# The order of VectorE's work in token attention, and the preparation of its first chunk

## The chip, the cores and the metric

One core of a Trainium2 chip runs the whole program. Its engines are TensorE (matrix products, with the weight load as a separate step), VectorE, ScalarE, GpSimd and SyncE; each runs its own list of instructions in order, and the lists are tied together by semaphores that count up. Transfers are started by SyncE, and those that scatter rows by GpSimd. The metric is the time of one execution on the device in microseconds (us).

## The reference, cut to what matters

The input is 16 images of 128 channels and 16x16 pixels. Three blocks follow one another:

```python
x = conv_block(x)                      # attention over the images, batch norm, relu, conv3x3 (Wc), + x
t = tokens(x)                          # 16 images x 256 pixels, 128 features
z = layer_norm(t)
sq, sk, rv = z @ wq_s * scale, z @ wk_s, z @ wv_r          # 8 search heads, 2 retrieval values, d = 16
search = softmax(sq @ sk.T)                                # per image and head: 256 x 256
retrieved = search @ rv                                    # two values per head
gate = softmax over the two of (rq . (retrieved @ wk_ret))
t = t + (sum over the two of gate * retrieved) @ w_out
z2 = layer_norm(t)
top2 of z2 @ Wg over 8 experts, softmax of the two         # routing
t = t + sum over the two of share * silu(z2 @ W1[e]) @ W2[e]
```

## The kernel before, in words

The 4096 tokens are cut into 8 chunks of 512 (two images each). Everything up to the relu comes first and is not touched. Then `token_attention` runs: for chunk g it convolves (`conv_taps`, nine taps, three products each since every operand is split into a high and a low part), adds the input (`add_conv`, VectorE), turns the sum to tokens (`head_turn`), normalises it (`norm_stats`, `normalise`), turns it back, and makes keys, queries and token products (`head_k`, `head_q`, `head_tokens`). Keys and queries go through memory (`qk_rows`, the "bounce") and come back laid out by head (`k_stack`, `q_stack`; six and three transfers for each of the two images), all issued by SyncE in `stack`.

The order of all engines is written out by hand in `body(g)`, one per chunk, with the same step names on every engine. A body has two halves, one for each image b of chunk g, of eight steps s (one head each). In a step TensorE makes `shifted_scores(g, b, s)` of this image and `scores` of the image that comes next; VectorE takes the maximum of each row of these scores (`row_max`, L1280). TensorE has two banks for `scores`, so scores s waits for row maximum s-2. After the eight steps VectorE splits the maxima in high and low (`split_max`, last instruction L1293), TensorE turns them (`turn_max`, L1605), VectorE and ScalarE place them as four extra rows of `q_stack` (`place_max`, L1298), and only then can the next half's shifted scores start. The exponent is ScalarE's; `retrieve` on TensorE multiplies by the values.

Between the row maxima, VectorE does the rest of its work in a fixed order. In the first half of body g (from chunk 2 on; chunk 1 has no routing yet):

- s = 1, 2, 3: `retrieve` parts 0, 1, 2 of chunk g-1 (the gate of the two values; part 2 writes `o_tok`, L1330 and L1334). TensorE needs `o_tok` at its step 4 for `tail_turn` (L1655), and through it the output projection.
- s = 2, 3, 4: `route` parts 0, 1, 2 of chunk g-2 (choice of two experts; L1359 to L1384), each behind the `retrieve` part of that step.
- s = 5: `add_attention` (L1341); s = 6: `norm_stats`; s = 7: `normalise_t2`.

In the second half: `row_max` of the next chunk's first image; behind the first one `add_conv(g + 2)` (L1242), which TensorE needs at its step 1 for `head_turn` (L1557); `retrieve` of chunk g at steps 1, 4, 5; statistics and normalisation at 3 and 4; at step 7 `place(g - 2)` (L1389 to L1408: six small instructions that turn the rank of each token among its expert's tokens into the row it is scattered to), then `split_max`. GpSimd waits for what `place` wrote (`rows_ready`) and scatters eight tiles of rows per chunk (L973). TensorE's `turn_max` at the end of this half writes the bank that `place` reads first, and waits for that (`spot_read`).

Body 6 has no convolution left, body 7 is written out apart (`last_body`). At the end the experts run, once all rows are scattered.

Ahead of body 0 stands the preparation of chunk 0: `stack(0, 0)` on SyncE, `scores(0, 0, s)` on TensorE with the same two banks, and `row_max(0, 0, s)`, with `add_conv(2)` behind the fourth. TensorE has the last tap of chunk 2's convolution behind its first scores. ScalarE's images 12 to 15 (`image_pair` 6 and 7) and VectorE's `low(12)` to `low(15)` stand ahead of the scores; the convolution of chunk 6 needs them four bodies later.

Of the kernel before, what the change touches and what calls it, by code (L numbers as in the profile page):

```python
# [22 lines left out]
PIX = HW * HW  # L23
# [683 lines left out]
def token_attention(nc, ctx, block, sb, sem, bank, pad_h, pad_l, resid, virt, ident, wc_h, wc_l, norm_a, norm_b, power, wq, wk,  # L707
# [170 lines left out]

    def chunk(tensor, g):
        return tensor[:, bass.ds(g * CH, CH)]  # L880

    @block.sync
    def _(sp):
        def stack(g, ring):
# [3 lines left out]
            def bounce(first, signal):  # L888

                sp.dma_start(qk_rows[bass.ds(g, 1), first:first + 2].rearrange("g n c t -> c (g n) t"),  # L890
                             f32(qk[:, first:first + 2, :])).then_inc(signal, 16)

            def fill_k(b):
                at = slice(b * PIX, (b + 1) * PIX)
                for slot, n in enumerate((0, 0, 1)):
                    src = qk_rows[bass.ds(g, 1), n, :, at].rearrange("g (p a r) t -> a r (g p) t", p=NP, a=2)
                    for a in range(2):
                        row = 32 * slot + D * a
                        sp.dma_start(f32(k_stack[row:row + D, ring, a:S:2, at]), src[a]).then_inc(stacked[b], 16)

            def fill_q(b):
                at = slice(b * PIX, (b + 1) * PIX)
                for slot, n in enumerate((2, 3, 2)):
                    src = qk_rows[bass.ds(g, 1), n, :, at].rearrange("g (p r) t -> r (g p) t", p=NP)
                    sp.dma_start(f32(q_stack[32 * slot:32 * slot + 32, ring, :, at]), src
                                 ).then_inc(stacked[b], 16)

            sp.wait_ge(k_ready, g + 1)
            bounce(0, k_bounced)
            sp.wait_ge(q_ready, g + 1)  # L910
            bounce(2, q_bounced)
            sp.wait_ge(k_bounced, 16 * (g + 1))
            fill_k(0)
            sp.wait_ge(q_bounced, 16 * (g + 1))
            fill_q(0)
            fill_k(1)
            fill_q(1)
# [4 lines left out]
        stack(0, 0)  # L922
# [75 lines left out]
    def _(act):  # L998
# [182 lines left out]

        keep_t(0)
# [4 lines left out]
        keep_tok(0, 0, 0)  # L1187
        keep_tok(0, 1, 0)
        image_pair(6)
        split_zt(1)  # L1190
# [23 lines left out]
    def _(dve):  # L1214
# [63 lines left out]
        def row_max(g, b, s):  # L1278
            dve.wait_ge(s_done, 2 * S * g + S * b + s + 1)
            nc.vector.tensor_reduce(s_max[:, :, s], ps_s[s % 2][:, :].rearrange("p (a j) -> p a j", a=2), AX.X,  # L1280
                                    ALU.max).then_inc(max_done, 1)
# [104 lines left out]
        def place(u, ring, src=ps_x):  # L1386
# [798 lines left out]
```

## Time and profile before

| what | value |
|---|---|
| time, median of 3 runs | 685.08 us (684.0 to 688.95) |
| the profiled execution | 685.38 us, span of the profile 683.6 us |
| mean granted TensorE clock | 0.927 of full speed |
| TensorE matmul busy | 566.0 us (83%) |
| VectorE busy | 475.9 us (70%) |
| ScalarE busy | 333.1 us (49%) |
| GpSimd busy | 262.6 us (38%) |
| first shifted scores of body 0 | 191.95 us |
| turns of `t_chunk` in bodies 1, 2, 3, 4 and 5 | 243.18, 280.30, 319.65, 357.59 and 395.47 us |
| first product of the experts | 500.40 us |

The profile is one execution. Its span is 1.78 us shorter than the time of that execution, which is 0.30 us above the median. Engines are named PE (TensorE), DVE (VectorE), ACT (ScalarE), POOL (GpSimd) and SPq (SyncE issuing transfers). In a timeline a row gives the start, the duration, engine, line, operation, what it writes and reads, and in brackets how long the engine was idle before it and what released it. DVE instructions overlap a little at their ends: a row maximum lasts 0.69 us, but the next instruction can start some 0.6 us after it. In a view by stretches each engine's busy time is followed by the number of its instructions.

### The profile page before, as it was taken

What the parts mean: (1) busy time and instruction counts of PE and PEld (TensorE: products, weight loads), DVE (VectorE), ACT (ScalarE), POOL (GpSimd) and SP (SyncE); (2) the same over time, 40 slices, a digit from 0 to 9 for tenths busy, and PEclk for the clock granted to TensorE, in tenths of its full rate; (3) what the DMA queues carried; (4) which work ended last, traced back from release to release, by engine and by line L of the source; (5) the groups of instructions that cost most, each with busy time, mean ns of one, the idle gap of its engine ahead of it and who ended that gap; (6) DMA issues with size and microseconds to landing.
All of it is one profiled execution on the core that took longest, in us unless ns stands there. A gap on an engine that the chain in (4) does not pass through costs nothing. (4 is left out here: it accounts for less than half of the span.)

```text
span 683.6 us, 10705 instructions
## 1 busy us (share of the span) xinstructions
PE 566.0 (83%) x3180; PEld 439.7 (64%) x3180; DVE 475.9 (70%) x1227; ACT 333.1 (49%) x718; POOL 262.6 (38%) x328
## 2 busy tenths in 40 slices
PE   5999999849788988979898887876169999999910
PEld 4888888636565767666666665654058888888810
DVE  6886774855557777777878778785537767767715
ACT  3322302233356465554636355544148888888800
POOL 3245443458000100141413314247603666666660
PEclk9999999959879999999999999998569999999965
DMA  7994145649531405041230505001278777776109
GB/s 262 365 347 145 57 170 185 203 164 372 153 116 39 155 1 155 1 151 36 96 92 31 157 3 184 9 25 48 76 251 293 234 243 230 246 235 221 51 6 363
DMA packets 55224, 105.46 MB, mean 154 GB/s; under 512 B 8744, under 2 KB 21689, under 8 KB 55040
## 3 DMA queue, kind: packets, MB, share of 16 engines
q1 hardware_dynamic: 50176, 96.24, 42.6%
q0 software_dynamic: 4992, 8.54, 3.6%
q8 instruction: 26, 0.43, 0.3%
q14 instruction: 30, 0.25, 0.1%
HBM read 58.15 MB, written 48.42 MB: 156 GB/s over the span
## 5 line engine op out<-in xcount | busy, mean ns | idle before, releaser
L1949 POOL DMA_INDIRECT y_slots<-virt,pad_l x92 | 95.7, 1041 | 72.5 <-DVE virt L2001 49.5
L1280 DVE TENSOR_REDUCE s_max<-bank 128x2 f32<-128x512 f32 x128 | 87.4, 689 | 40.3 <-PE bank L1596 39.8
L1059 ACT ACTIVATE s_expd<-bank 128x512 f32<-128x512 f32 x128 | 76.9, 602 | 53.5 <-PE bank L1617 52.3
L973 POOL DMA_INDIRECT x_slots<-rows,slot_of x64 | 63.1, 986 | 55.9 <-DVE rows L1408 38.3
L937 POOL TENSOR_TENSOR ln_rstd<-ln_var,power 128x4 f32<-128x4 f32 x17 | 17.4, 1026 | 173.4 <-DVE ln_var L1256 173.4
L1989 DVE TENSOR_TENSOR k_stack<-virt,k_stack 128x512 fp32r<-128x512 f32 x92 | 63.4, 689 | 24.9 <-ACT k_stack L1968 24.2
L1632 PE MATMUL bank<-s_expd,rvx 128*64 128x256 f32 x512 | 70.5, 397 | 1.5 <-ACT s_expd L1059 1.0
L61 PE MATMUL bank<-pad_h,u_h 128*128 128x512 f32 x144 | 59.9, 416 | 8.4 <-DVE pad_l L399 8.4
L1617 PE MATMUL bank<-q_stack,k_stack 100*128 100x256 f32 x256 | 61.8, 325 | 5.0 <-DVE q_stack L1298 5.0
L1968 ACT ACTIVATE k_stack<-virt 128x512 fp32r<-128x512 f32 x92 | 58.2, 633 | 10.1 <-PE bank L63 7.2
L1963 ACT ACTIVATE virt<-bank 128x512 f32<-128x512 f32 x92 | 55.0, 597 | 14.3 <-PE bank L63 13.9
L1596 PE MATMUL bank<-k_stack,q_stack 96*128 96x256 f32 x256 | 55.5, 303 | 3.9 <-DMA q_stack<-qk_rows 2.3
L63 PE MATMUL bank<-pad_h,u_l 128*128 128x512 f32 x144 | 58.0, 403 | 0.0
L62 PE MATMUL bank<-pad_l,u_h 128*128 128x512 f32 x144 | 57.9, 402 | 0.0
L1617 PEld LDWEIGHTS bank<-q_stack,k_stack 100*128 100x128 f32 x256 | 43.0, 199 | 18.0 <-DVE q_stack L1298 7.0
L1596 PEld LDWEIGHTS bank<-k_stack,q_stack 96*128 96x128 f32 x256 | 42.5, 204 | 6.2 <-DVE s_max L1280 2.8
L1632 PEld LDWEIGHTS bank<-s_expd,rvx 128*64 128x64 f32 x512 | 31.5, 138 | 22.6 <-ACT s_expd L1059 5.1
L1066 ACT ACTIVATE ret_f<-bank 128x256 f32<-128x256 f32 x64 | 24.4, 382 | 39.8 <-PE bank L1632 39.8
L61 PE MATMUL bank<-k_stack,pad_h 128*128 128x512 f32 x92 | 40.5, 440 | 0.0
L1984 DVE TENSOR_TENSOR k_stack<-bank,k_stack 128x512 fp32r<-128x512 f32 x23 | 15.9, 692 | 30.5 <-ACT k_stack L1958 30.5
L61 PEld LDWEIGHTS bank<-pad_h,u_h 128*128 128x128 f32 x144 | 27.8, 193 | 14.3 <-issue 8.3
L62 PE MATMUL bank<-k_stack,pad_h 128*128 128x512 f32 x92 | 36.7, 399 | 0.0
(260 smaller groups left out, 1321.8 us busy)
## 6 DMA issues: line engine op xcount, KB each, us to landing
x_slots<-blank SPq DMA_DIRECT2D x8, 2112.0 KB, 17.3
pad_h<-w_split SPq DMA_DIRECT2D x23, 512.0 KB, 4.4
q_stack<-w_split SPq DMA_DIRECT2D x23, 512.0 KB, 5.7
qk_rows<-qk SPq DMA_DIRECT2D x16, 512.0 KB, 3.0
k_stack<-qk_rows SPq DMA_DIRECT2D x96, 64.0 KB, 2.4
q_stack<-qk_rows SPq DMA_DIRECT2D x48, 128.0 KB, 2.6
pad_l<-x_slots SPq DMA_DIRECT2D x23, 264.0 KB, 5.2
e_raw<-in_w SPq DMA_DIRECT2D x16, 256.0 KB, 3.0
```

The lines of the kernel that those rows point to most:

```text
L61: pe.matmul(out, w_h, x_h, start=start, stop=False)
L62: pe.matmul(out, w_h, x_l, start=False, stop=False)
L63: return pe.matmul(out, w_l, x_h, start=False, stop=stop)
L973: pool.indirect_dma_start(out=x_slots[:, :], out_offset=bass.IndirectOffsetOnAxis(ap=slot_of[:, ring, k, j:j + 1], axis=0), in_=rows[:, ri ...
L1059: nc.scalar.activation(expd[:, s % 4].rearrange("p a i -> p (a i)"), ps_st[s % 2][:, :], ACT.Exp).then_inc(exp_done, 1)
L1280: nc.vector.tensor_reduce(s_max[:, :, s], ps_s[s % 2][:, :].rearrange("p (a j) -> p a j", a=2), AX.X, ALU.max).then_inc(max_done, 1)
L1596: last = pe.matmul(ps_s[s % 2][:, i * PIX:(i + 1) * PIX], q_stack[0:96, ring, s // 2, at + i * P:at + (i + 1) * P], k_stack[0:96, ring, s, ...
L1617: last = pe.matmul(ps_st[s % 2][:, i * PIX:(i + 1) * PIX], k_stack[0:100, ring, s, at + i * P:at + (i + 1) * P], q_stack[0:100, ring, s // ...
L1632: last = pe.matmul(ps_pv[p % 2][h * RF:(h + 1) * RF, 0:PIX], rvx[:, ring, 2 * b + a, :], expd[:, 2 * (p % 2) + h, a, :], start=(a == 0), s ...
L1949: pool.indirect_dma_start(out=y_slots[:, :], out_offset=bass.IndirectOffsetOnAxis(ap=ids, axis=0), in_=y_rows[:, t % 2, j, :], in_offset=N ...
L1968: nc.scalar.activation(hid_h[:, f], hid[:, f], ACT.Copy).then_inc(hid_high, 1)
L1989: nc.vector.tensor_tensor(hid_l[:, f], hid[:, f], f32(hid_h[:, f]), ALU.subtract).then_inc(hid_ready, 1)
```

## The change

Five things, all in `token_attention`:

1. First half of a body: `retrieve` part 2 of chunk g-1 moves from step 3 to step 2, directly behind part 1. The three parts of `route` move from steps 2, 3, 4 to steps 4, 5, 6.
2. Second half: `add_conv` moves ahead of the first `row_max`.
3. `place` is cut in two. `place_spots` (its first instruction, the one that reads the bank) stays at step 7; `place_rows` (the other five) goes behind `split_max` and `place_max`, to the end of the body.
4. Chunk 0: its scores use four banks instead of two (`ps_s + ps_st`); TensorE makes the last tap of chunk 2's convolution ahead of them, and VectorE `add_conv(2)` ahead of all its row maxima. `low(12)` to `low(15)` move into steps 2 to 5 of body 0.
5. Chunk 0's transfers: SyncE bounces and lays out the keys alone (both images, 1 + 12 transfers); ScalarE bounces the queries between its two `keep_tok` and lays them out behind `split_zt(1)` (1 + 6 transfers), ahead of `image_pair(6)`.

```diff
     @block.sync
+        def first_stack():
+            sp.wait_ge(k_ready, 1)
+            bounce(sp, 0, 0, k_bounced)
+            sp.wait_ge(k_bounced, 16)
+            fill_k(sp, 0, 0, 0)
+            fill_k(sp, 0, 0, 1)
...
-        stack(0, 0)
+        first_stack()
         stack(1, 1)
...
     @block.scalar
+        def bounce_first_q():
+            act.wait_ge(q_ready, 1)
+            bounce(act, 0, 2, q_bounced)
+        def stack_first_q():
+            act.wait_ge(q_bounced, 16)
+            act.wait_ge(stack_init, 2 * S + 1)
+            fill_q(act, 0, 0, 0)
+            fill_q(act, 0, 0, 1)
...
         keep_tok(0, 0, 0)
+        bounce_first_q()
         keep_tok(0, 1, 0)
+        split_zt(1)
+        stack_first_q()
         image_pair(6)
-        split_zt(1)
         image_pair(7)
...
     @block.vector
-        def place(u, ring, src=ps_x):
+        def place_spots(u, src=ps_x):
...
+        def place_rows(u, ring):
             at, n = tiles_of(u), count_of(u)
             dve.wait_ge(spot_read, 4 * u + 1)
...
+                if stage == FIRST and s in (2, 3, 4, 5):
+                    low(10 + s)
                 if stage != FIRST:
-                    if s in (1, 2, 3):
+                    if s in (1, 2):
                         retrieve(g - 1, 1, s - 1)
+                    if s == 2:
+                        retrieve(g - 1, 1, 2)
                     if s == 5:
                         add_attention(g - 1)
...
-                if g >= 2 and s in (2, 3, 4):
-                    route(g - 2, ring, s - 2)
+                if g >= 2 and s in (4, 5, 6):
+                    route(g - 2, ring, s - 4)
...
             for s in range(S):
+                if stage == MIDDLE and s == 0:
+                    add_conv(g + 2)
                 if stage != LAST:
                     row_max(g + 1, 0, s)
-                if stage == MIDDLE and s == 0:
-                    add_conv(g + 2)
...
                 if g >= 2 and s == 7:
-                    place(g - 2, ring)
+                    place_spots(g - 2)
...
                 place_max(g + 1, 0, 1 - ring)
+            if g >= 2:
+                place_rows(g - 2, ring)
...
-        low(12)
-        low(13)
         low_zt(1)
-        low(14)
-        low(15)
+        add_conv(2, ps_pv[0])
         for s in range(S):
-            row_max(0, 0, s)
-            if s == 3:
-                add_conv(2, ps_pv[0])
+            row_max(0, 0, s, first_banks)
...
     @block.tensor
-            need(pe, max_done, 2 * S * g + S * b + s - 1)
+            need(pe, max_done, 2 * S * g + S * b + s + 1 - len(banks))
...
-        conv_taps(2, range(4, 8), ps_pv[0])
+        conv_taps(2, range(4, 9), ps_pv[0])
         head_k(1)
         for s in range(S):
-            scores(0, 0, s, 0)
-            if s == 0:
-                conv_taps(2, range(8, 9), ps_pv[0])
+            scores(0, 0, s, 0, first_banks)
```

`last_body` and what follows it keep their order; there `place` is only written as its two parts one behind the other.

## Rows read from the trace of the kernel before

**Rows 1.** Stretch, length, busy PE, PEld, DVE, ACT, POOL, PEclk, DMA: bodies 2, 4.
```profile
280.30:319.65 39.35, 35.03 (x227) 26.33 (x227) 29.97 (x99) 19.80 (x51) 10.87 (x13) 0.96 0.27 82
357.59:395.47 37.88, 33.54 (x226) 24.95 (x227) 29.79 (x99) 19.69 (x51) 10.88 (x13) 1.00 0.28 85
```

**Rows 2.** Timeline of TensorE: its waits for VectorE in bodies 1, 2 and 6.
```profile
228.30 0.63 PE L1655 MATMUL bank<-ident,o_tok 128*128 128x128 f32 x4 [0.72 <-DVE o_tok L1334]
...
265.42 0.63 PE L1655 MATMUL bank<-ident,o_tok 128*128 128x128 f32 x4 [1.82 <-DVE o_tok L1334]
...
276.52 0.38 PE L1605 MATMUL bank<-ident,m_split 128*128 128x128 f32 x2
...
280.30 0.65 PE L1557 MATMUL bank<-ident,t_chunk 128*128 128x128 f32 x4 [0.69 <-DVE t_chunk L1242]
...
292.91 0.41 PE L1605 MATMUL bank<-ident,m_split 128*128 128x128 f32 x2 [1.61 <-DVE m_split L1293]
...
440.57 0.41 PE L1605 MATMUL bank<-ident,m_split 128*128 128x128 f32 x2 [0.75 <-DVE m_split L1293]
```

**Rows 3.** Chain that ended last: the first scatter of the last body.
```profile
461.10 1.04 POOL x_slots L973
```

**Rows 4.** Timeline of VectorE in the first half of body 2.
```profile
262.62 0.18 DVE L1369 TENSOR_REDUCE best<-logits 128x4 f32<-128x32 f32 x1
...
263.73 0.69 DVE L1280 TENSOR_REDUCE s_max<-bank 128x2 f32<-128x512 f32 x1
264.34 0.41 DVE L1330 TENSOR_TENSOR prod<-prod,ret 128x256 f32<-128x256 f32 x1
...
265.19 0.18 DVE L1372 SCALAR_TENSOR_TENSOR other<-hot,logits 128x32 f32<-128x32 f32 x1
...
268.20 0.69 DVE L1280 TENSOR_REDUCE s_max<-bank 128x2 f32<-128x512 f32 x1 [0.37 <-PE bank L1596]
269.25 0.69 DVE L1341 TENSOR_TENSOR resid<-bank,resid 128x512 f32<-128x512 f32 x1 [0.35 <-PE bank L1661]
270.50 0.69 DVE L1280 TENSOR_REDUCE s_max<-bank 128x2 f32<-128x512 f32 x1 [0.57 <-PE bank L1596]
...
272.97 0.69 DVE L1280 TENSOR_REDUCE s_max<-bank 128x2 f32<-128x512 f32 x1 [0.38 <-PE bank L1596]
...
275.57 0.21 DVE L1293 TENSOR_TENSOR m_split<-s_neg,m_split 128x16 fp32r<-128x16 f32 x1
```

**Rows 5.** Busy time by stretch: the first half of body 6, without convolution.
```profile
412.00:425.00 13.00, 10.66 (x80) 7.57 (x78) 12.18 (x45) 7.20 (x21) 5.48 (x7) 1.00 0.70 215
```

**Rows 6.** Timeline of VectorE in the second half of body 2.
```profile
283.55 0.69 DVE L1280 TENSOR_REDUCE s_max<-bank 128x2 f32<-128x512 f32 x1 [1.00 <-PE bank L1596]
...
291.28 0.18 DVE L1389 TENSOR_TENSOR spot<-bank,first_row 128x32 f32<-128x32 f32 x1
...
292.18 0.17 DVE L1289 TENSOR_SCALAR s_neg<-s_max 128x16 f32<-128x16 f32 x1
```

**Rows 7.** Timeline: VectorE's first row maximum of body 6; GpSimd behind a scatter.
```profile
410.28 0.69 DVE L1280 TENSOR_REDUCE s_max<-bank 128x2 f32<-128x512 f32 x1 [0.83 <-PE bank L1596]
...
455.26 1.04 POOL L937 TENSOR_TENSOR ln_rstd<-ln_var,power 128x4 f32<-128x4 f32 x1 [4.46 <-DVE ln_var L1256]
```

**Rows 8.** Timeline of all engines in the preparation of chunk 0.
```profile
176.68 0.63 ACT L1030 ACTIVATE zt_h<-zt 128x512 fp32r<-128x512 f32 x1
...
177.62 1.37 SPq L905 DMA_DIRECT2D q_stack<-qk_rows  x3
...
181.41 0.60 PE L1596 MATMUL bank<-k_stack,q_stack 96*128 96x256 f32 x2 [2.34 <-DMA q_stack<-qk_rows]
...
189.45 0.17 DVE L1289 TENSOR_SCALAR s_neg<-s_max 128x16 f32<-128x16 f32 x1
...
190.82 0.37 ACT L1053 ACTIVATE q_stack<-bank 4x256 fp32r<-4x256 f32 x1 [11.91 <-PE bank L1605]
```

**Rows 9.** Busy time by stretch: the start of the second half of body 6.
```profile
428.00:430.00 2.00, 2.00 (x12) 1.77 (x10) 1.58 (x5) 1.38 (x4) 0.87 (x3) 0.50 0.00 0
```

More of the change, by code:

```diff
@@ L877, in max_bank, with bounce, fill_k @@
         return ps_x if stage in (FIRST, MIDDLE) else ps_conv
+    first_banks = ps_s + ps_st
     def chunk(tensor, g):
         return tensor[:, bass.ds(g * CH, CH)]
+    def bounce(queue, g, first, signal):
+        queue.dma_start(qk_rows[bass.ds(g, 1), first:first + 2].rearrange("g n c t -> c (g n) t"),
+                        f32(qk[:, first:first + 2, :])).then_inc(signal, 16)
+    def fill_k(queue, g, ring, b):
+        at = slice(b * PIX, (b + 1) * PIX)
+        for slot, n in enumerate((0, 0, 1)):
+            src = qk_rows[bass.ds(g, 1), n, :, at].rearrange("g (p a r) t -> a r (g p) t", p=NP, a=2)
+            for a in range(2):
+                row = 32 * slot + D * a
+                queue.dma_start(f32(k_stack[row:row + D, ring, a:S:2, at]), src[a]).then_inc(stacked[b], 16)
@@ L882, in _, with fill_q @@
+    def fill_q(queue, g, ring, b):
+        at = slice(b * PIX, (b + 1) * PIX)
+        for slot, n in enumerate((2, 3, 2)):
+            src = qk_rows[bass.ds(g, 1), n, :, at].rearrange("g (p r) t -> r (g p) t", p=NP)
+            queue.dma_start(f32(q_stack[32 * slot:32 * slot + 32, ring, :, at]), src
+                            ).then_inc(stacked[b], 16)
     @block.sync
     def _(sp):
-        def stack(g, ring):
[L888 to L906, printed above, removed]
@@ L908, in stack @@
+        def first_stack():
[4 more added lines that the diff above has]
+            fill_k(sp, 0, 0, 1)
+        def stack(g, ring):
             sp.wait_ge(k_ready, g + 1)
-            bounce(0, k_bounced)
+            bounce(sp, g, 0, k_bounced)
             sp.wait_ge(q_ready, g + 1)
-            bounce(2, q_bounced)
+            bounce(sp, g, 2, q_bounced)
             sp.wait_ge(k_bounced, 16 * (g + 1))
-            fill_k(0)
+            fill_k(sp, g, ring, 0)
@@ L1474, in last_body @@
             normalise_t2(g - 1, 0)
-            place(g - 2, ring)
+            place_spots(g - 2)
+            place_rows(g - 2, ring)
             for part in range(3):
@@ L1479, in last_body @@
                 route(g - 1, 0, part)
-            place(g - 1, 0)
+            place_spots(g - 1)
+            place_rows(g - 1, 0)
             add_attention(IMAGE_A)
@@ L1518, in _ @@
         route(IMAGE_A, 1, 2)
-        place(IMAGE_A, 1, ps_s[0])
+        place_spots(IMAGE_A, ps_s[0])
+        place_rows(IMAGE_A, 1)
         for part in range(3):
             route(IMAGE_B, 1, part)
-        place(IMAGE_B, 1, ps_s[1])
+        place_spots(IMAGE_B, ps_s[1])
+        place_rows(IMAGE_B, 1)
         dve.wait_ge(list_sums, 1)
@@ L1587, in head_tokens, with scores @@
                 last.then_inc(tok_done, 1)
-        def scores(g, b, s, ring):
+        def scores(g, b, s, ring, banks=ps_s):
             if s == 0:
                 pe.wait_ge(stacked[b], STACK * (g + 1))
-            need(pe, max_done, 2 * S * g + S * b + s - 1)
+            need(pe, max_done, 2 * S * g + S * b + s + 1 - len(banks))
             at = b * PIX
             for i in range(2):
-                last = pe.matmul(ps_s[s % 2][:, i * PIX:(i + 1) * PIX],
+                last = pe.matmul(banks[s % len(banks)][:, i * PIX:(i + 1) * PIX],
                                  q_stack[0:96, ring, s // 2, at + i * P:at + (i + 1) * P],
```

11 lines of the change are left out of this document (6 added, 5 removed).

## The prediction

> **What bounds the kernel now.** I read the views from the outside in. First the busy time of a whole body, from one turn of `t_chunk` to the next [rows 1]: body 4 lasts 37.88 us, in which TensorE works for 33.54 and VectorE for 29.79. The reader is to see that TensorE sets the pace and that at most its idle time, 4.34 us, can be won in a body. Body 2 is longer by 1.47 us at a mean clock of 0.96; that is a matter of the clock, below.
>
> Second, TensorE's waits in the timeline [rows 2]. In body 2 there are three, each for VectorE: 1.82 us for `o_tok`, 0.69 for `t_chunk`, 1.61 for the split maxima that end the body. Together 4.12, nearly the whole idle time. The same three stand, to 0.03 us, in bodies 2, 3, 4 and 5; body 1, which has no routing yet, waits 0.72 for `o_tok`, and body 6 waits 0.75 for the maxima that end it. Between 265.42 and 280.30 TensorE waits for nothing: it reaches the turn of the maxima at 276.52 without a wait.
>
> Third, the chain that ended last: attention ends with the scatters of GpSimd, and the chain enters them at 461.10 [rows 3], when VectorE in `last_body` has placed chunk 5. Behind it lie 8 + 8 + 4 + 4 scatters and the experts, none of which the change touches. So whatever VectorE and TensorE save before `last_body` goes to the end one to one.
>
> **Retrieval ahead of routing.** In body 2 `retrieve` part 2 starts at 264.34, behind routing's part 0 and a row maximum that begin at 262.62 [rows 4]. With both out of the way `o_tok` comes 1.72 us earlier, and TensorE, which waits 1.82, starts its turn at about 263.70.
>
> Not all of it is kept, because what stood ahead now stands behind, nearer to the end of the half. From 262.62 on VectorE has part 2 (264.34 to 265.19, 0.85), two row maxima that are ready (263.73 to 264.34, 0.61 each) and routing's part 0 (262.62 to 263.73, 1.11): it is through at 265.80. The next row maximum hangs on TensorE and comes 1.72 earlier than now, at 266.48; `add_attention` likewise at 267.53. After that routing's parts 1 and 2 fill what was waiting. So of the four waits 0.37, 0.35, 0.57 and 0.38 [rows 4], 1.67 in all, some 0.94 stays (the first two, the first of them longer: 0.59 + 0.35), and 0.73 goes. The split ends at 275.78 now, 0.73 earlier is 275.05, and 0.15 for the signal (o_tok's own delay) puts `turn_max` at 275.2, where TensorE alone would be there at 276.52 - 1.72 = 274.80. The half gets 1.32 shorter by this count; since neighbouring DVE instructions overlap by some 0.09 at each wait that goes, I take 1.4. Bounds: 1.72 if VectorE is never late, 0 if it becomes the bound, as body 6 shows it: there VectorE works 12.18 of 13.00 us [rows 5], and its order of work changes nothing, so I count no gain in body 6. Four bodies (2 to 5) give 5.6. In body 1 only a row maximum (0.61) leaves the front of part 2, against a wait of 0.72: 0.6. Sum 6.2.
>
> **Convolution's sum first.** It waits only for the convolution's last tap, which ends before TensorE begins the half; VectorE is then idle until the first scores arrive. The row maximum behind it is some 0.2 us late, but the scores that wait for it come two steps later. TensorE's 0.69 goes in bodies 1 to 5. That it lasts to the end of the half is seen at the fourth row maximum, where VectorE waits 1.00 for TensorE [rows 6]; from there on VectorE runs through to the split, so the chain simply starts earlier. 5 x 0.69 = 3.45.
>
> **Ranks in two parts.** From 291.28 to 292.18 `place` holds up the split by 0.90 [rows 6]. The spots stay (about 0.15 of it); 0.75 leaves, and TensorE's wait behind it is 1.61 (bodies 2 to 5) or 0.75 (body 6), so all of it counts: 5 x 0.75 = 3.75. The five moved instructions then stand ahead of the next body's first row maximum. What hides them is VectorE's wait there, 0.83 [rows 7]; without it each body would lose 0.75. The scatters start about 1.5 us later in a body. Behind them GpSimd waits 4.46 us for the next statistics [rows 7], and in the other bodies longer: hidden too.
>
> **Chunk 0.** Now the first scores start at 181.41 and the split at 189.45 [rows 8], 8.04 us, in which a convolution tap and `add_conv` stand between eight row maxima on two banks. With four banks and both of them ahead, VectorE has eight maxima in a row: 0.60 for the first product + 7 x 0.61 + 0.73 = 5.60, a gain of 2.4. The tap and the sum are hidden by the wait for the transfers (2.34 us of TensorE). The start depends on the third query transfer. SyncE issues three in 1.37 us from 177.62, so the third starts at 178.53 and TensorE 2.88 later. ScalarE comes to its three when `zt_h` is written, at 177.31 now; the bounce ahead delays it by an issue (0.46), image pair 6, now behind it, gives time back: it lies between 176.7 and 177.8, and I take 177.1. Third transfer 178.0, scores 180.9, 0.5 earlier. No row here has a transfer issued by ScalarE. Sum 2.9; bounds 4 (nothing but VectorE's eight maxima, at once) and 1.55 (the rival below). ScalarE's images 12 to 15 come some 5 us later (six issues of 0.46 and the wait for the bounce); what hides that is its 11.91 us of idle time ahead of `place_max` at 190.82 [rows 8]. The four `low` go into VectorE's waits for TensorE in body 0, of the kind and size of rows 4; not hidden they would cost 4 x 0.4 (an estimate from the 0.69 of a full-width row, for half the width).
>
> By the Trainium skill (Perfetto Trace Analysis, DMA Instruction — HWDGE) the block that generates descriptors is shared by the issuing engines and locked for one instruction at a time. By it the gain of this part would be the 1.55 of the rival below; no run here shows it yet.
>
> **The clock.** Body 2 has a mean granted clock of 0.96, body 4 with the same waits and the same work 1.00, and body 2 takes 1.47 longer [rows 1]: TensorE fell to the lower level, 1.2 GHz, for a while. The same is seen in body 6, behind the waits of its middle: 0.50 for 2 us [rows 9]. With half of the 1.61 of body 2 gone I count half of the 1.47: 0.7.
>
> **Sum.** 6.2 + 3.45 + 3.75 + 2.9 + 0.7 = 17.0. The profiled execution took 685.38 (span 683.6 and 1.78 around it), so 668.4; it lies 0.3 above the median, within the spread of the runs shown.
>
> **The rivals.** (a) VectorE becomes the bound of the first half, as in body 6: each `o_tok` wait turns into a wait for the split, and the 6.2 is lost: 674.6. For it speaks that VectorE's slack falls to under 1 us; against it that the row maximum and `add_attention` still wait for TensorE in my count.
>
> (b) The two issuing engines hinder each other in the preparation. SyncE's second image of keys and ScalarE's queries would be issued in turn, at 0.46 each: the third query transfer starts not at 178.0 but near 179.4, the scores near 182.25. 1.35 is lost: 669.8.
>
> (c) Not faster at all: the clock. Without its term the gain is 16.3. A fall costs 1.4 to 1.5. If TensorE fell to 1.2 GHz behind the turn of the maxima in each half of bodies 0 to 6, 14 times, of which two are there already (body 2, and body 6 [rows 9]), 12 more would cost 16.8 to 17.6: 685.9 to 686.7. From the 12th additional fall on, the change doesn't pay. Against it: but for the new 0.4 at `turn_max` no wait of TensorE gets longer, and body 4 stays at 1.00 [rows 1] with the longest of them.
>
> (d) The rewriting doesn't do what it says, if TensorE's waits are held by something that only ends together with VectorE: ScalarE's token copies for `o_tok`, for instance. Then only ranks and preparation remain, 6.65: 678.7.
>
> **How the numbers follow.** Forecast 0.66, (a) 0.15, (b) 0.11, (c) 0.03, (d) 0.05. The time is that of the forecast, 668.4. The range reaches down to 663: all of the 1.72 four times over (1.3), the preparation's better bound (1.1) and a clock without falls there and in body 2 (some 3). Upward it takes in (b) and (a), with both together at 676. A measurement of this kernel can tell about 1%, 6.9 us, from no change. Faster than 678.2: 0.91 (the forecast, (a), (b) and little of (d)), within 1%: 0.07, slower: 0.02.
>
> **What the profile would show.** The turns of `t_chunk` from body 2 to 5 at distances of about 35.0 us instead of 37.9. TensorE's wait for `o_tok` near 0.1, for `t_chunk` 0, for the maxima at the end of a body near 0.8, and a new one of some 0.4 at `turn_max` in the first half; were that one near 1.8, (a) is right. The row maximum behind the five moved instructions with a wait near 0.1. The first scores near 181 and the split 5.6 later; scores past 182 speak for (b). `last_body`'s first scatter near 444. What would make it wrong most: a new wait on VectorE in the middle of a half, for a transfer or for ScalarE, which stands in none of these rows.

## The result and the profile after

| what | before | after |
|---|---|---|
| time, median | 684.54 us (4 runs, 683.32 to 688.95) | 670.42 us (4 runs, 669.33 to 670.85) |
| ratio | | 0.9753, 95% interval 0.9711 to 0.9796 |
| the profiled execution, its span | 685.38 and 683.6 us | 670.67 and 668.9 us |
| mean granted clock | 0.927 | 0.924 |
| turn of `t_chunk` in bodies 1 to 5 | see above | 240.42, 275.44, 310.33, 345.28, 380.15 us |
| first product of the experts | 500.40 us | 484.74 us |

14.1 us faster, where 17.0 were forecast; the time lies in the range. The three parts in VectorE's order did what was forecast; chunk 0's preparation did not, and the clock had a much larger say than half of one fall.

Busy time by stretch of the kernel after, bodies 2 and 4 (columns as in [rows 1]): 39.35 and 37.88 us have become 34.9 with the same work, TensorE idle 1.35 instead of 4.3, both at 1.00.

```profile
275.44:310.33 34.89, 33.54 (x229) 24.84 (x228) 29.63 (x99) 19.70 (x53) 10.94 (x13) 1.00 0.30 92
345.28:380.15 34.87, 33.49 (x228) 24.85 (x227) 29.62 (x99) 19.70 (x53) 10.69 (x13) 1.00 0.30 92
```

Timeline of TensorE after, answering [rows 2]: body 1's `o_tok`, then body 2's four places, then the end of body 6. The waits of 0.72, 1.82, 0.69 and 1.61 are now 0.24, 0.34, none and 0.84; `turn_max` in the middle (272.44) lists none. It still starts 0.15 behind the end of VectorE's split (272.07 + 0.22) and 0.48 behind the start of the product before it, where the kernel before has 0.27: VectorE holds it up by some 0.2.

```profile
226.38 0.63 PE L1686 MATMUL bank<-ident,o_tok 128*128 128x128 f32 x4 [0.24 <-DVE o_tok L1358]
...
261.12 0.63 PE L1686 MATMUL bank<-ident,o_tok 128*128 128x128 f32 x4 [0.34 <-DVE o_tok L1358]
...
272.44 0.41 PE L1636 MATMUL bank<-ident,m_split 128*128 128x128 f32 x2
...
275.44 0.60 PE L1588 MATMUL bank<-ident,t_chunk 128*128 128x128 f32 x4
...
287.22 0.41 PE L1636 MATMUL bank<-ident,m_split 128*128 128x128 f32 x2 [0.84 <-DVE m_split L1317]
...
425.13 0.41 PE L1636 MATMUL bank<-ident,m_split 128*128 128x128 f32 x2
```

Timeline of VectorE after, first half of body 2 and start of body 3, answering [rows 4] and [rows 7]: two waits stay (0.74 and 0.35), the next row maximum follows without one, and neither does the row maximum behind the five moved instructions (289.41) wait. The split of the maxima ends at 272.29.

```profile
263.91 0.69 DVE L1304 TENSOR_REDUCE s_max<-bank 128x2 f32<-128x512 f32 x1 [0.74 <-PE bank L1627]
264.95 0.69 DVE L1365 TENSOR_TENSOR resid<-bank,resid 128x512 f32<-128x512 f32 x1 [0.35 <-PE bank L1692]
...
266.89 0.69 DVE L1304 TENSOR_REDUCE s_max<-bank 128x2 f32<-128x512 f32 x1
...
272.07 0.22 DVE L1317 TENSOR_TENSOR m_split<-s_neg,m_split 128x16 fp32r<-128x16 f32 x1
...
289.20 0.17 DVE L1435 TENSOR_TENSOR rows<-rows,gap_e 128x4 f32<-128x4 f32 x1
289.41 0.69 DVE L1304 TENSOR_REDUCE s_max<-bank 128x2 f32<-128x512 f32 x1
```

Chain that ended last, after: it enters the scatters at 445.59, 15.51 earlier than in [rows 3].

```profile
445.59 1.05 POOL x_slots L983
```

Preparation of chunk 0 after, timeline of all engines, answering [rows 8]: SyncE issues keys and ScalarE queries side by side, the scores wait for a query transfer, and the split follows 5.45 us later (8.04 before).

```profile
174.18 5.53 SPq L895 DMA_DIRECT2D k_stack<-qk_rows  x12
175.91 2.83 ACTq L901 DMA_DIRECT2D q_stack<-qk_rows  x6
...
181.28 3.88 PE L1627 MATMUL bank<-k_stack,q_stack 96*128 96x256 f32 x16 [2.08 <-DMA q_stack<-qk_rows]
...
186.73 0.17 DVE L1313 TENSOR_SCALAR s_neg<-s_max 128x16 f32<-128x16 f32 x1
```

**A caution on comparing two profiles.** Work ahead of the change isn't equally long in two executions: the split of chunk 0's queries (`low_q`) starts at 171.94 in the profile before and at 171.28 after, and between 168.93 and 171.94 over all kernels shown here. So distances are compared, or shifts between two places. The row of `low_q` in the timelines of VectorE before and after:

```profile
171.94 0.69 DVE L1276 TENSOR_TENSOR qk<-bank,qk 128x512 fp32r<-128x512 f32 x1
...
171.28 0.69 DVE L1300 TENSOR_TENSOR qk<-bank,qk 128x512 fp32r<-128x512 f32 x1
```

The shift of after against before, step by step:

| place | shift, us | so the part gave, us | forecast |
|---|---|---|---|
| `low_q` of chunk 0 (ahead of the change) | -0.66 | 0.66, not the change's | 0 |
| `turn_max` of chunk 0 | -2.71 | 2.05 preparation | 2.9 |
| end of body 0 | -1.44 | -1.27 | 0 |
| body 1: `o_tok`; bodies 2 to 5: first halves | | 0.48; 1.26, 1.36, 1.38, 1.37 = 5.85 retrieval | 0.6 + 5.6 |
| body 3: the fall of the clock that is gone | | 1.46 | 0.7 |
| bodies 1 to 5: `t_chunk` | | 0.84, 0.78, 0.81, 0.79, 0.81 = 4.03 sum first | 3.45 |
| ends of bodies 1 to 5 | -16.15 | 0.06, 0.83, 0.82, 0.83, 0.83 = 3.37 ranks | 3.0 |
| body 6 | -15.44 | -0.10 and -0.61 | 0 and 0.75 |
| first scatter, experts' first product, end | -15.51, -15.66, -14.7 | -0.74 | 0 |

(Body 3's first half gave 2.82; of that 1.46 is its fall of the clock before, which made the stretch from the end of body 2 to the turn of `o_tok` 11.88 us long, against 10.42 in body 4.) What is missing stands in three places: body 0, body 6 and the start of the experts. All three show the clock.

Busy time by stretch, after: the first half of body 0 in its part at 0.50 and its rest, the second half of body 6, the experts' first 10 us.

```profile
189.24:195.26 6.02, 6.02 (x24) 4.37 (x24) 3.69 (x6) 2.66 (x5) 0.00 (x0) 0.50 0.28 108
195.26:203.50 8.24, 8.04 (x60) 5.90 (x59) 4.90 (x11) 5.50 (x15) 0.00 (x0) 0.98 0.78 187
409.57:425.13 15.56, 14.38 (x91) 10.67 (x92) 10.42 (x27) 8.04 (x21) 0.87 (x3) 0.78 0.01 1
484.74:494.74 10.00, 8.50 (x31) 6.79 (x31) 3.46 (x5) 6.00 (x11) 0.00 (x0) 0.61 0.91 290
```

The same four stretches before:

```profile
191.95:195.16 3.21, 3.21 (x12) 2.92 (x13) 1.38 (x2) 1.36 (x3) 0.00 (x0) 0.50 0.00 0
195.16:204.93 9.77, 9.57 (x71) 6.75 (x71) 5.97 (x11) 6.81 (x18) 0.00 (x0) 0.99 0.67 200
425.62:440.57 14.95, 13.02 (x91) 9.67 (x92) 11.12 (x32) 8.42 (x22) 0.87 (x3) 0.89 0.03 9
500.40:510.40 10.00, 8.49 (x35) 6.89 (x36) 3.69 (x6) 6.04 (x11) 0.00 (x0) 0.72 0.95 309
```

Body 0 starts 2.71 earlier after the change, but in these two profiles the granted clock comes back from 1.2 to 2.4 GHz at the same moment (near 195.2). So TensorE does twice as much of the half at the lower level (6.02 us instead of 3.21), and the half takes 14.26 instead of 12.98 us. The size differs from profile to profile: in the six kernels below and here that have the new preparation and no products added in it (after, prep_only, second_held, sync_all, fill_tail, route_late) the half takes 13.51 to 14.27 us, in the six with the old one (before, retr_only, conv_only, rank_only, order_only, retr_fill) 12.97 to 14.21.

### The profile page after: what moved, and what is told of

Same layout as the page of the kernel before. It is cut to its first block and busy times, and to the rows that moved or that the text cites. A ratio compares the mean times of both kernels' runs of the same rounds, so it can differ in the third digit from the quotient of the medians.

```text
span 668.9 us, 10706 instructions
## 1 busy us (share of the span) xinstructions
PE 565.4 (85%) x3180; PEld 438.6 (66%) x3180; DVE 474.3 (71%) x1227; ACT 333.6 (50%) x718; POOL 262.1 (39%) x328
## 5 line engine op out<-in xcount | busy, mean ns | idle before, releaser
L1304 DVE TENSOR_REDUCE s_max<-bank 128x2 f32<-128x512 f32 x128 | 85.9, 687 | 24.3 <-PE bank L1627 23.6
L1627 PE MATMUL bank<-k_stack,q_stack 96*128 96x256 f32 x256 | 54.1, 300 | 2.7 <-DMA q_stack<-qk_rows 2.1
```

The lines of the kernel that those rows point to most:

```text
L1304: nc.vector.tensor_reduce(s_max[:, :, s], banks[s % len(banks)][:, :].rearrange("p (a j) -> p a j", a=2), AX.X, ALU.max).then_inc(max_done, 1)
L1627: last = pe.matmul(banks[s % len(banks)][:, i * PIX:(i + 1) * PIX], q_stack[0:96, ring, s // 2, at + i * P:at + (i + 1) * P], k_stack[0:96 ...
```

## The experiments

**Each part alone.** Four kernels, each the kernel before with one part of the change. Their edits are the parts of the diff above.

```diff
retr_only
-                    if s in (1, 2, 3):
+                    if s in (1, 2):
                         retrieve(g - 1, 1, s - 1)
+                    if s == 2:
+                        retrieve(g - 1, 1, 2)
...
-                if g >= 2 and s in (2, 3, 4):
-                    route(g - 2, ring, s - 2)
+                if g >= 2 and s in (4, 5, 6):
+                    route(g - 2, ring, s - 4)
conv_only: add_conv(g + 2) ahead of row_max(g + 1, 0, s)
rank_only: place_spots at step 7, place_rows at the end of the body
prep_only: first_stack, bounce_first_q, stack_first_q, first_banks, low(12) to low(15) in body 0
```

> The kernel before with the first part of the change alone (retrieval's last part behind its second, routing at steps 4 to 6). Theory: each part takes away its own wait of TensorE and they add up; by the trace of after this one is worth 0.5 us in body 1 and 1.3 to 1.4 us in each of bodies 2 to 5, so about 5.9 us: 678.6 us against 684.5, ratio 0.991. TensorE's wait for o_tok falls from 1.82 to 0.2 us in body 2. Rival: VectorE is then the bound and what is won in the first half is waited for at the next t_chunk or at the end of the body: under 2 us, ratio above 0.997, and the waits of 0.69 and 1.61 us grow by what the first one lost.

> The kernel before with the second part alone (the convolution's sum ahead of the first row maximum of the second half). Theory: 0.8 us in each of bodies 1 to 5, 4.0 us in all: 680.5 us, ratio 0.994; the wait for t_chunk is gone and the wait at the end of the body stays at 1.6 us. Rival: VectorE reaches the end of the half no sooner, the 0.7 us come back at the split maxima, which then wait 2.3 us: ratio 1.000.

> The kernel before with the third part alone (ranks placed in two parts). Theory: 0.8 us in each of bodies 2 to 5 and up to 0.75 in body 6, 3.3 to 4.0 us in all: 681 us, ratio 0.995; the wait at the end of the body falls from 1.61 to 0.84 us. Rival: the five instructions, now ahead of the next body's first row maximum, cost there what they gave: TensorE's wait for o_tok grows from 1.82 to 2.5 us, ratio 1.000.

> The kernel before with the fourth and fifth parts alone (four banks, the tap and the sum ahead of the scores, queries issued by ScalarE). The prediction gave 2.9 us: 681.6, ratio 0.9957. Theory from the trace of after: the first shifted scores come 2.1 us earlier (and 0.65 by something else that stands ahead of the change), but the clock stays at 0.50 until the same moment near 195 us, so body 0 gives back 1.3: 0.8 us left, 683.7 us, ratio 0.9988. Rival: body 0's loss in after comes from the four instructions low, moved into its steps; then the clock's part is small and DVE shows waits of TensorE for row maxima behind low.

| kernel | median, us | ratio, 95% interval | low stretches in bodies 1 to 6, up to the middle of body 6 |
|---|---|---|---|
| before | 685.69 (35 runs) | | from 294 |
| retr_only | 682.68 | 0.9945 (0.9917 to 0.9974) | from 328, 366, 403 |
| conv_only | 683.33 | 0.9944 (0.9917 to 0.9971) | from 292, 329, 404 |
| rank_only | 681.54 | 0.9932 (0.9904 to 0.9961) | from 375 |
| prep_only | 685.21 | 0.9996 (0.9962 to 1.003) | from 291, 329, 407 |

Each of the three parts of VectorE's order takes its own wait away, as the theories said: in retr_only the wait for `o_tok` is 0.23, in conv_only none for `t_chunk`, in rank_only 0.84 at the ends; no rival's sign is seen. Their gains, 3.8, 3.8 and 4.7 us by the ratios, are near what was expected for two, and short for retrieval (5.9). TensorE's timeline shows what took time from it in the profiled execution, though conv_only's profile has as many low stretches and its gain isn't short: one profile doesn't stand for ten runs. This is the end of body 3 in retr_only: the wait for the split maxima that this part leaves in place, and right behind it products of 512 columns that take 0.63 us instead of 0.40.

```profile
327.32 0.41 PE L1607 MATMUL bank<-ident,m_split 128*128 128x128 f32 x2 [1.62 <-DVE m_split L1293]
...
328.24 0.63 PE L62 MATMUL bank<-zt_l,wk_h 128*128 128x512 f32 x1
```

The stretch behind that wait in the view by stretches of retr_only, at 0.54:

```profile
327.80:331.50 3.70, 3.67 (x12) 3.13 (x13) 1.62 (x4) 2.08 (x5) 2.83 (x3) 0.54 0.14 41
```

And in rank_only, behind a wait of 1.81 for `o_tok` that this part leaves in place, at 0.50:

```profile
375.50:378.50 3.00, 3.00 (x10) 2.51 (x10) 2.05 (x9) 0.60 (x1) 1.92 (x2) 0.50 0.81 236
```

prep_only is no faster than before. Its first half of body 0 takes 13.54 us (12.98 before): longer, as the theory had it, but by 0.56 and not 1.3. The clock came back at 192.0 there, not near 195. By stretches, prep_only:

```profile
192.00:192.50 0.50, 0.50 (x8) 0.24 (x4) 0.50 (x2) 0.00 (x0) 0.00 (x0) 1.00 0.51 193
```

What the theory got right is the distance from `low_q`: the clock comes back 23.1 us behind its start in prep_only, 23.4 before and 24.2 after. So by the end of body 0 prep_only is 1.06 us ahead of before (45.90 against 46.96 behind `low_q`); then its profile has three falls up to the middle of body 6 where before has one, which takes more than that. That the four `low` are to blame, its rival, falls with fill_prep below.

**The three parts together, and the clock by itself.** The first kernel has all three parts of VectorE's order and the old preparation. The second is retr_only with products into a bank that is free, in the wait at the end of a body.

```diff
retr_fill
+        def fill(n, dst):
+            for _ in range(n):
+                pe.matmul(dst[:, :], wc_h[:, 0, :], wc_h[:, 0:4, :], start=True, stop=True)
...
+            if stage != LAST and g:
+                pe.wait_ge(max_done, 2 * S * (g + 1) + S - 1)
+                fill(4, ps_s[0])
             if stage != LAST:
                 need(pe, spot_read, 4 * (g - 2) + 1)
                 turn_max(g + 1, 0)
```

> The kernel before with the three parts in VectorE's order together (retrieval, convolution's sum, ranks), chunk 0's preparation as before. Alone they gave 3.0, 2.4 and 4.1 us at the medians, 9.5 in sum. Theory (the clock ties them together): alone, each leaves waits of 1.6 to 1.8 us in place, behind which TensorE falls to 1.2 GHz in three, three and one of the bodies 2 to 6; together no wait over 0.9 us is left there and none of them falls: 13.5 us faster, 672 us, and no low stretch between 200 and 400 us. Rival: the parts just add up: 676 us; the difference to after is then chunk 0's.

> The retrieval part alone, with four products on TensorE that nobody reads in the wait at the end of bodies 1 to 6 (into a bank whose last reader is done). Without them TensorE fell to 1.2 GHz at 328, 366 and 403 us, each time just behind the wait of 1.62 us. Theory: filled, the waits are followed by no fall: the three low stretches go, each worth 1.35 us, and the time goes from 682.7 to 678.6 us. Rival: the falls have nothing to do with the waits; they stay, 682.7, or the added products delay the turn of the maxima and cost up to 1 us.

order_only: 670.05 us, ratio 0.9766 (0.9714 to 0.9819). The three ratios multiply to 0.982, which lies just above that interval: together the parts give more than one by one, some 4 us, a rough size since the product has an interval of its own. retr_fill: 677.68 us, ratio 0.9895 (0.9839 to 0.9951), against 682.68 without the four products; three of its four runs lie below the lowest of retr_only's ten. The same wait is 0.50 now, and the products behind it run at 0.40:

```profile
324.08 1.20 PE L1559 MATMUL bank<-wc_h 128*128 128x512 f32 x4
325.78 0.41 PE L1611 MATMUL bank<-ident,m_split 128*128 128x128 f32 x2 [0.50 <-DVE m_split L1293]
...
326.62 0.39 PE L62 MATMUL bank<-zt_l,wk_h 128*128 128x512 f32 x1
```

Over bodies 1 to 5 both kernels, order_only here, are at 1.00 throughout, where [rows 1] has body 2 at 0.96:

```profile
200.00:400.00 200.00, 190.15 (x1285) 140.32 (x1286) 165.63 (x527) 115.65 (x300) 43.03 (x54) 1.00 0.28 86
```

From the end of body 3 to the middle of body 6, retr_fill wins 3.76 us on retr_only (the shift between the two grows from 1.54 to 5.30) and nothing else was changed: three falls, 1.25 us each. So it is shown that filling the waits keeps the clock up. That a large part of what the three parts gain beyond their product is the clock's follows from it, but isn't shown by a run of its own. What decides whether such a wait is followed by a fall isn't settled: from body 2 to the start of body 6 the kernel before has waits of 1.6 and 1.8 us in each body, and one of them is followed by a fall.

**Chunk 0's transfers.** second_held keeps the second image's transfers back, sync_all has SyncE issue all; both keep the four banks.

```diff
second_held
             fill_k(sp, 0, 0, 0)
+            sp.wait_ge(stacked[0], STACK)
             fill_k(sp, 0, 0, 1)
+            fill_q(sp, 0, 0, 1)
...
             fill_q(act, 0, 0, 0)
-            fill_q(act, 0, 0, 1)
sync_all
-        first_stack()
+        stack(0, 0)
...
-        bounce_first_q()
...
-        stack_first_q()
```

> The changed kernel, but the nine transfers of chunk 0's second image are issued by SyncE only when the first image's nine have landed. In after the six query transfers took 4.2 to 5.1 us from issue to landing and the keys 3.9 to 5.3, against 2.5 to 2.8 and 2.1 to 2.8 before. Theory: the transfers of the two images share the queues' bandwidth in flight; with the second image held back the first one's land in about 3 us and the scores start 1 to 1.5 us earlier than now, measured from the end of the queries' split: 8.5 us behind it instead of 10.0. Rival: ScalarE's own queue is slow or the issuing hinders itself; then the landing stays above 4 us and the start where it is.

> The changed kernel with all of chunk 0's transfers issued by SyncE in the old order (four banks and the order of tap, sum and row maxima stay). Theory: ScalarE's part of the issuing wins nothing, since its earlier issue is lost again in flight: the scores start within 0.3 us of after's, measured from the end of the queries' split (9.5 to 10.1 us behind it; 9.5 before, 10.0 after), with landings near 2.5 us again. Rival, as the prediction had it: the start is 0.5 us later than after's, or more.

Profiled at 668.62 and 668.72 us (one execution each). The time from issue to landing of the query transfers stands in the view of the tile `q_stack` between 168 and 184 us. Before:

```profile
DMA to landing us min/median/max: 2.5/2.8/2.8
```

After:

```profile
DMA to landing us min/median/max: 4.2/4.7/5.1
```

second_held:

```profile
DMA to landing us min/median/max: 2.5/2.6/2.6
```

sync_all:

```profile
DMA to landing us min/median/max: 2.5/2.6/2.7
```

First scores, counted from the start of `low_q`: 9.47 us before, 10.00 after, 9.19 with the second image held, 9.44 with SyncE alone. (The 8.5 expected of second_held was counted from the end of that instruction and the 10.0 from its start; by one measure the start comes 0.81 earlier, a little less than the 1 to 1.5 expected.) So the queries' flight was lengthened by the second image's transfers: without them two issuers side by side land in 2.6 us. It takes both, though. In sync_all the second image's keys are issued right behind the first image's queries, from 176.86, and those still land in 2.5 to 2.7. Whether the generation of the transfers or their data was the narrow place, these runs don't tell. And ScalarE's issuing of both images, the fifth part of the change, by itself made the start 0.56 later than SyncE alone. All profiles of the two kinds agree: the first scores stand 9.36 to 9.49 us behind `low_q` in the six kernels with the old preparation, and 9.96 to 10.44 in the five in which ScalarE issues both images' queries (after, prep_only, fill_prep, fill_tail, route_late).

**The clock in the preparation and ahead of the experts.** Products nobody reads, in TensorE's idle time, into `ps_pv[1]` and `ps_x`.

```diff
fill_prep
+        fill(7, ps_pv[1])
         for s in range(S):
             scores(0, 0, s, 0, first_banks)
+        fill(9, ps_pv[1])
         turn_max(0, 0)
+        fill(3, ps_pv[1])
fill_tail: behind the last product of the experts' list
+        fill(26, ps_x)
```

> The changed kernel with 19 products added on TensorE in chunk 0's preparation that nobody reads (7 ahead of the first scores, 9 behind the eighth, 3 behind the turn of the maxima, into a bank that is free), so that TensorE isn't idle there. Theory (the clock): the granted clock then stays at 1.00, the low stretch of 181.9 to 195.5 is gone, body 0's first half takes 11.6 us instead of 14.3 and the scores and the turn some 0.7 less: 3.3 us faster than after, 667.1 us. Rival: the clock falls there whatever TensorE does, or the added products delay the scores: 670.4 or up to 1 us more.

> The changed kernel with 26 products added on TensorE behind the list of the experts, in the 10 us in which it waits for the last scattered rows, again into a bank that nobody reads. In after the experts run at 0.50 for their first 7.7 us (484.7 to 492.5), before for 5 us (500.4 to 505.5). Theory: with the clock at 1.00 from the start the experts end 2 to 3 us sooner: 668 us. Rival: their first tiles are bound by the transfers of weights and rows: no change, 670.4; or the added products end too late and cost 1 us.

fill_prep: 667.11 us (four runs, 665.89 to 667.53, all below the lowest of after), ratio 0.9738 (0.9703 to 0.9774). The first half of body 0 has 1.00 throughout and takes 11.51 us, as expected. The four `low` are still in it, and TensorE is idle for 0.20 us of it: they cost nothing that can be seen. By stretches:

```profile
188.25:199.76 11.51, 11.31 (x82) 8.30 (x82) 8.32 (x17) 8.16 (x20) 0.00 (x0) 1.00 0.50 159
182.80:186.00 3.20, 3.20 (x9) 2.62 (x10) 2.79 (x7) 0.00 (x0) 0.00 (x0) 0.50 0.00 0
```

But one fall stayed, at 183, and in it the nine products lasted into the turn of the maxima, which came 7.07 us behind the first scores instead of 6.11. From `low_q` to the end of the half it is 2.14 us less than after (30.08 against 32.22), where 3.3 were expected; where the rest of the medians' difference (3.3) comes from, this profile doesn't show.

fill_tail: 670.0 us, ratio 0.9784 (0.9746 to 0.9821): no change that can be told. TensorE's timeline shows the 26 products end 2.55 us before the rows come:

```profile
472.70 7.80 PE L1588 MATMUL bank<-wc_h 128*128 128x512 f32 x26
483.05 1.12 PE L2077 MATMUL bank<-ident,pad_l 128*128 128x128 f32 x4 [2.55 <-DMA pad_l<-x_slots]
```

By stretches the clock was up at 1.00 in this wait and fell again as the experts began (0.66 over their first 10 us, 0.61 after):

```profile
476.20:483.00 6.80, 4.30 (x19) 3.19 (x17) 0.00 (x0) 0.00 (x0) 1.71 (x2) 1.00 0.39 122
483.05:493.05 10.00, 8.49 (x32) 6.87 (x33) 3.56 (x6) 6.02 (x11) 0.00 (x0) 0.66 0.90 294
```

**Body 6.** Its first half got no shorter, and TensorE's wait for the split maxima grew from 0.93 to 2.65 us. route_late takes routing out of this half in body 6 alone.

```diff
-                if g >= 2 and s in (4, 5, 6):
+                if g >= 2 and stage != LAST_BUT_ONE and s in (4, 5, 6):
                     route(g - 2, ring, s - 4)
...
+                if stage == LAST_BUT_ONE and s in (1, 2, 3):
+                    route(g - 2, ring, s - 1)
```

> The changed kernel with routing moved into the second half in body 6 alone (steps 1 to 3). Theory: in body 6, where no convolution is left, VectorE is the bound of the first half: TensorE waits 2.65 us for the split maxima there, and the low stretch of 410.6 to 417.4 follows that wait. 3.1 us of VectorE's work less in this half: the wait falls below 0.6 us (2.2 us won), the low stretch goes or halves (1 to 1.4 us won): 3 to 3.5 us faster than after, 667 us. Rival: the second half then becomes VectorE's, and the end of body 6 comes no sooner: 670.4.

TensorE's timeline in body 6 of route_late, at the split maxima and in the second half's steps:

```profile
407.54 0.41 PE L1638 MATMUL bank<-ident,m_split 128*128 128x128 f32 x2 [0.40 <-DVE m_split L1317]
...
415.54 0.50 PE L1629 MATMUL bank<-k_stack,q_stack 96*128 96x256 f32 x2 [1.72 <-DVE s_max L1304]
```

And the stretch behind it:

```profile
417.00:423.80 6.80, 6.80 (x36) 5.44 (x35) 3.23 (x8) 2.43 (x7) 0.00 (x0) 0.50 0.00 0
```

Half a hit. The wait falls to 0.40 and the first half is 2.25 us shorter, so VectorE's 12 us of work did set it. But in the second half a row maximum stands behind routing's second part, TensorE waits 1.72 for it, and the clock falls right there: the half takes 18.15 us instead of 15.56, and of the 2.25 us nothing is left in the profile: the whole body is 0.34 us longer than after (670.97 us, the slowest of four; median 668.12, ratio 0.9738, 0.9686 to 0.9791, not to be told from after).

**A version from all of it.** The second image held, 4, 5 and 3 products in the preparation, 34 ahead of the experts, routing late in body 6.

> The changed kernel with what the runs so far speak for: chunk 0's second image held back until the first has landed, 4, 5 and 3 products to keep TensorE busy in the preparation, 34 behind the experts' list (26 ended 2.6 us before the experts began, and the clock had fallen again by then), routing of body 6 in its second half. Theory by parts: 0.8 + 2.9 + 2 + 3 us: 661.7 us, experts at full clock from their first product. Rival for the tail: the experts' first tiles are bound by the transfers, or the clock rises late and the 34 products end behind the rows: 663 to 665. Rival for the preparation: the filler that is shorter leaves the fall at 183 us: 663.

664.95 us (six runs, 662.14 to 667.51), ratio 0.9687 (0.9642 to 0.9731): faster than both kernels, each of the six runs below the lowest of after, 5.5 us at the medians. It is 3.3 us short of the 661.7 expected. Its profile (667.41 us, the second slowest of the six) shows where. Chunk 0's parts came, 3.7 expected: the end of body 0 stands 42.76 us behind `low_q`, against 46.18 after. There is no fall from 170 to 400 us. The experts run at 1.00 from their first product; from there to the end of the span it takes 182.3 us against 184.2 after, near the 2 expected. But routing late in body 6, 3 expected, gave nothing: TensorE waits 1.73 for a row maximum in the second half, the clock falls behind it (412 to 419), and the body is 0.4 us longer than after. And a long fall in `last_body` (439.5 to 449.5) cost about 2.3 by the experts' first product. By stretches:

```profile
170.00:400.00 230.00, 216.65 (x1439) 159.70 (x1439) 184.92 (x565) 131.55 (x336) 47.06 (x59) 1.00 0.31 97
483.31:493.31 10.00, 7.85 (x39) 6.16 (x40) 4.73 (x7) 7.51 (x14) 0.00 (x0) 1.00 0.91 296
439.50:449.50 10.00, 9.86 (x42) 6.63 (x41) 4.42 (x19) 4.42 (x13) 6.71 (x9) 0.50 0.10 35
```

## Why the prediction was right, and where not

- **Retrieval ahead of routing: right.** 5.85 us against 6.2; `o_tok` waits 0.22 to 0.34, not 1.82; of VectorE's four waits the first two stay, 1.09 us against the 0.94 of the count. Rival (a) would have shown 1.8 at `turn_max`; no wait is listed there. The small one that the count had in its place is there all the same: the turn of `o_tok` comes 1.5 to 1.6 sooner, the turn of the maxima 1.26 to 1.38, since it starts when the split is through. In body 6 nothing was won, as forecast, and for the reason forecast (route_late): the 1.61 won at `o_tok` comes back as a wait of 2.65 instead of 0.93 for the split maxima.
- **Convolution's sum first: right, a little low.** 4.03 against 3.45: the wait of 0.69 goes, and some 0.1 more in each body. In body 2 the turn started 1.09 us behind the start of the product before it and now starts 0.24 behind: 0.85 sooner, of which the row lists 0.69 as a wait.
- **Ranks in two parts: right in bodies 2 to 5** (3.31 against 3.0), where the five instructions are hidden as said. Wrong in body 6: instead of 0.75 won, 0.61 lost, since the second half ran longer at 1.2 GHz (0.78 against 0.89 in the stretch). The low stretch of 410.5 to 417.5 begins behind the wait of 2.65 that the moved routing left there. So the argument against rival (c), that no wait but the one at `turn_max` gets longer, did not hold in body 6.
- **Chunk 0: the mechanism of the split right, the size wrong.** The eight row maxima took 5.45 us (5.60 forecast). Two steps failed. First "TensorE 2.88 later": ScalarE's third query transfer was issued even earlier than forecast (5.6 us behind the start of `low_q`, where 178.0 was 6.1), but it flew 4.2 us or more, not 2.88, since the duration was taken from a row with one issuer. Rival (b) had the effect and not the cause: issuing did not take turns, SyncE's twelve took 0.46 each and ScalarE's six 0.47, side by side. By the Trainium skill (DMA: Bandwidth & Descriptors, Issuing engines are not separate DMA queues) transfers of all issuers run on the same 16 DMA engines, and two issuers save only the time of issuing; this trace agrees as far as it goes (4.7 against 2.8 us to landing). Second, the sum took for granted that what the preparation wins reaches the end. Body 0 gave 1.27 of it back, because TensorE's clock came back no earlier. Of 2.9 us some 0.8 is left in the trace (by the end of body 0, counted from `low_q`, 0.6 to 1.5 in the four profiles with this preparation and no products added there), and in the times nothing that can be told (prep_only 0.9996; order_only without it 0.9766, after 0.9753).
- **The clock: mis-sized, in both directions.** Forecast 0.7, from half of one fall. In the two profiles it gave 1.46 in body 3 and took 1.27 in body 0, some 1.4 in body 6 (0.61 lost where 0.75 was to be won) and 1.0 at the experts' start. From kernel to kernel it gave more: the profiles of the parts alone, which leave waits of 1.6 to 1.8 us, have one to three falls up to the middle of body 6, all three together none in bodies 1 to 5, and order_only gained some 4 us beyond the product of its parts. The prediction's fault was to size a thing that differs from run to run from a single execution. The kernel before, in the eleven runs measured with order_only, ran at mean clocks of 0.913 to 0.935, in 691.6 to 682.4 us; the kernel after, in its four runs, at 0.924 to 0.926.
- **The total.** Of 17.0 us forecast, 13.4 were the order's; the trace has 12.5 of them (5.85 + 4.03 + 3.37 - 0.71). The other 3.6, chunk 0's and the clock's, shrank to 1.5 (2.05 + 1.46 - 1.27 - 0.74). That makes 14.0, as the medians say; the trace's 14.7 has the 0.66 of the work ahead in it. That the two agree so closely is partly luck, since the kernel before alone spreads over 9 us. That the forecast of 17.0 came as near as 3 us is luck in part too: convolution and the fall of body 3 gave more than forecast, and made up for some of what chunk 0, body 6 and the start of the experts lacked.

## What to carry to other kernels

Where one engine paces a loop and waits for another, list its waits in one turn of the loop and order the other engine's work by when each result is needed: each wait was won nearly whole, and hardly anything of it was lost behind, but for the half in which VectorE had no time to spare (body 6), where all of it was. Count what TensorE's idle time does to the clock apart from the idle time itself, and over several runs, not one; a wait shortened to 0.2 to 0.9 us, as here, or filled with products nobody reads, can be worth as much again. That is no promise: in body 6 before the change the clock fell (427 to 431) behind two waits of 0.93 and 0.96. A transfer's duration from the trace holds for the company in which it flew: two issuers side by side won nothing here, holding back what isn't needed yet did.

## What was not expected of the hardware

The granted clock comes back late: behind chunk 0's preparation TensorE was busy without a pause for 6.0 us at 1.2 GHz after the change, 3.2 us before. Counted from `low_q`, in stretches of 0.1 us, the rise came 22.6 to 24.2 us later in the six profiles named above with the new preparation, and 23.4 to 23.9 in five of the six with the old one (26.3 in conv_only), though the first shifted scores came 17.2 to 18.7 us later in the new and 19.5 to 20.2 in the old. So part of the work made ready earlier was only done at the lower level. Why the rise comes there, and why it spreads, these runs don't show.

A wait of 1.6 to 1.8 us was followed by a fall in some bodies and not in others with the same wait, in the same execution. With waits of at most 0.96 us in bodies 1 to 5, none of eight profiles (after, order_only and the six kernels built on after) shows one there.

One cast of VectorE costs 0.59 us instead of 0.17 at the end of each first half in bodies 1 to 5, before and after the change alike. Timeline of VectorE and GpSimd after, body 2:

```profile
271.40 0.61 POOL L973 COPY rows<-rows 128x512 f32<-128x512 f32 x1 [1.33 <-DVE rows L1286]
271.45 0.59 DVE L1315 CAST m_split<-s_neg 128x16 fp32r<-128x16 f32 x1
...
286.69 0.18 DVE L1315 CAST m_split<-s_neg 128x16 fp32r<-128x16 f32 x1
```

It starts just behind a copy of GpSimd and ends with it; the same cast in the second half, where GpSimd is idle, takes 0.18. By the Trainium skill (SBUF — State Buffer, SBUF: two separate sides) the two engines share a pair of ports that one of them holds for a whole instruction; the trace agrees, also in the first halves of bodies 0 and 6, where no copy runs and the cast takes 0.17 to 0.18. No run moved the copy, so the cause is not shown. The cast stands on the path to `turn_max`; without the 0.4 TensorE could gain there the 0.2 or so by which the split holds it up, as an estimate from the starts of the rows; that wasn't tried.
